# Count matrix of a graph kernel: exact chunk counts through a ring of four slots, and the search for repeats gathered in 14 ranges

## The reference

```python
o = argsort(dst, stable=True)                    # so dst comes sorted, src not
x = x + gat(h, ..., src, dst)                     # sums over the edges of a node
W = zeros((256, 256)).at[src, dst].set(weight)    # edges inside 256 x 256; the last of equal ones wins
x = x + h @ W
x = x + sage(h, edge_index, ...)                  # segment sums of x[src] over dst
x = x + attention(h, edge_index, ...)             # sums exp(...) * h[dst] over src
```

## Time and profile before

| | |
|---|---|
| median of 3 runs | 2122.45 us |
| the profiled execution | 2122.24 us, its span 2120.4 us |
| TensorE matmul | 1728.6 us busy, 82% |
| VectorE | 1583.0 us, 75% |
| ScalarE | 1378.7 us, 65% |
| GpSimd | 303.5 us, 14% |
| changed stage | from about 31 to 319 us |

### The profile page before, as it was taken

One profiled execution on the slowest core, in us unless ns is written; L12 is line 12 of the kernel. 1 busy time (PEld: TensorE's weight loads), 2 busy tenths in 40 slices (PEclk: granted clock), 3 DMA queues, 4 the chain that ended last, 5 costly groups with the idle time before them and its releaser, 6 DMA issues. The chain is left out here.

```text
span 2120.4 us, 63580 instructions
## 1 busy us (share of the span) xinstructions
PE 1728.6 (82%) x21987; PEld 1375.2 (65%) x21987; DVE 1583.0 (75%) x3455; ACT 1378.7 (65%) x2350; POOL 303.5 (14%) x451
## 2 busy tenths in 40 slices
PE   4999985598998737899893699998989985488884
PEld 1333333588888627888883477775548984488883
DVE  7989987899999888999999522222332257899996
ACT  0246885999999659999995622221113354799986
POOL 2466511456500020000000000000000001100000
PEclk9999997799999878999997899999999998699997
DMA  2000000010101000010101200000001010000002
GB/s 84 5 1 2 3 2 27 14 40 28 40 27 40 2 27 30 28 40 27 40 27 50 90 8 0 0 0 7 1 20 36 20 61 14 8 21 28 21 22 99
DMA packets 34799, 54.96 MB, mean 26 GB/s; under 512 B 10668, under 2 KB 26240, under 8 KB 34432
## 3 DMA queue, kind: packets, MB, share of 16 engines
q1 hardware_dynamic: 31232, 51.64, 7.2%
q0 software_dynamic: 3328, 0.06, 0.1%
HBM read 43.19 MB, written 8.49 MB: 24 GB/s over the span
## 5 line engine op out<-in xcount | busy, mean ns | idle before, releaser
L1201 PE MATMUL ps<-R,M 128*128 128x132 f16 (+1 forms) x8640 | 827.1, 222 | 189.7 <-DVE M L1120 112.0
L1201 PEld LDWEIGHTS ps<-R,M 128*128 128x128 f16 x8640 | 763.0, 97 | 218.8 <-issue 115.0
L1075 ACT ACTIVATE Rm<-rows,cB 128x1280 bf16<-128x1280 f32 (+3 forms) x816 | 846.9, 1132 | 31.7 <-DVE Mn L1110 18.4
L1209 PE MATMUL ps<-HB,C 128*128 128x66 f16 x6400 | 590.2, 193 | 0.0
L1209 PEld LDWEIGHTS ps<-HB,C 128*128 128x128 f16 x6400 | 571.6, 97 | 0.0
L1120 DVE TENSOR_TENSOR M<-Rm,C 128x1280 f16<-128x1280 bf16 (+3 forms) x816 | 530.7, 674 | 36.9 <-ACT Rm L1075 29.4
L600 PE MATMUL acc<-ohc,ohl 128*128 128x420 f16 (+1 forms) x1161 | 246.3, 349 | 26.3 <-DVE ohl L564 23.6
L562 DVE TENSOR_SCALAR ohc<-cells,near 128x1280 f16<-128x1280 f16 x387 | 214.3, 554 | 27.9 <-PE acc L600 23.4
L1123 DVE SCALAR_TENSOR_TENSOR M<-rows,cN,C 128x1280 f16<-128x1280 f32 (+1 forms) x144 | 217.3, 1509 | 0.0
L600 PEld LDWEIGHTS acc<-ohc,ohl 128*128 128x128 f16 x1161 | 89.8, 98 | 174.9 <-DVE ohl L564 119.4
L1547 PE MATMUL psA<-R,C 128*128 128x512 f16 (+1 forms) x800 | 144.7, 331 | 9.6 <-DVEq L2036 3.7
(11 more groups left out here) (296 smaller groups left out, 2404.3 us busy)
## 6 DMA issues: line engine op xcount, KB each, us to landing
rows<-rowd SPq DMA_DIRECT2D x32, 640.0 KB, 4.0
rows<-rowd SPq DMA_DIRECT2D x16, 320.0 KB, 3.4
xd<-R SPq DMA_DIRECT2D x4, 640.0 KB, 2.9
xr<-xd SPq DMA_DIRECT2D x20, 128.0 KB, 2.1
xd<-HB SPq DMA_DIRECT2D x1, 2560.0 KB, 8.1
xr<-xd SPq DMA_DIRECT2D x5, 512.0 KB, 6.0
R<-in_x SPq DMA_DIRECT2D x1, 2432.0 KB
xr<-in_x SPq DMA_DIRECT2D x19, 128.0 KB, 2.0
```

Of the source, the lines that this page charges most:

```text
L1075: a.activation(Rm[:, s % SG, 0:wide(p)], rows[:, p % 2, 0:wide(p)], ACT.Relu, bias=cB[:, ds(h + s * nh, 1)]).then_inc(s_R, 1)
L1201: m = pe.matmul(region(p % 2, r), lhsT, rhs, start=first, stop=True, skip_group_check=True)
L1209: m = pe.matmul(both[:, :, cw:2 * cw], C[:, s * NP + p * W + r * P:][:, 0:P], VP[:, s, :, ds(h * cw, cw)], start=False, stop=True, skip_gr ...
```

## The change

Chunks go singly. The table holds the exact number of chunks of a range (three at least), a turn of the loop takes one chunk, and the buffers are a ring of RING = 4 slots whose number is worked out in registers as `(before + i) % RING`, with `before` the number of chunks of earlier ranges. TensorE takes two chunks ahead of the search. The searches are no longer one to a range: the first 14 ranges hold two each (28 in all), the other 26 none. The table of rounds has room for three turns of 28.

```diff
+RING = 4
+SEARCHED = [2] * 14
+NS = sum(SEARCHED)
+TURNS = -(-RND // NS)
...
-                ch(v.tensor_scalar(threes, threes, 1 / U3, 1 / U3, ALU.mult, ALU.add))
-                ch.wait()
-                ch(v.tensor_scalar(table[:, NW:2 * NW], threes, 2.0, None, ALU.max))
-                ch.wait()
-                ch(v.tensor_copy(threes, table[:, NW:2 * NW]))
-                ch.wait()
-                ch(v.scalar_tensor_tensor(table[:, 0:NW], threes, float(PACK), first, ALU.mult, ALU.add))
+                ch(v.tensor_scalar(counts, counts, 3.0, None, ALU.max))
+                ch.wait()
+                ch(v.scalar_tensor_tensor(table[:, 0:NW], counts, float(PACK), first, ALU.mult, ALU.add))
...
-            ohc = ph.sb("ohc", [P, U3, CELLS], f16)
-            ohl = ph.sb("ohl", [P, U3, P], f16)
+            ohc = ph.sb("ohc", [P, RING * CELLS], f16)
+            ohl = ph.sb("ohl", [P, RING * P], f16)
...
+            def slot_of(eng, step):
+
+                return nc.s_assert_within(step % RING, 0, RING - 1, skip_runtime_bounds_check_because="a remainder")
...
-                for q in range(NW):
+                for q in range(NS):
                     w = q % 2
                     with sp.Fori(0, turns) as i:
                         r = round_of(sp, q, i)
...
-                    with v.Fori(0, threes) as i:
-                        for u in range(U3):
-                            k = chunk(first + i * U3 + u, NG * P - 1)
-                            v.wait_ge(s_used, (before + i) * U3 + u + 1)
-                            v.tensor_scalar(ohc[:, u, :], cells[:, :], near[:, q % 2, ds(k, 1)], None,
-                                            ALU.is_equal).then_inc(s_oh, 1)
-                            v.tensor_scalar(ohl[:, u, :], lows[:, :], bT[:, ds(k, 1)], None,
-                                            ALU.is_equal).then_inc(s_oh, 1)
+                    with v.Fori(0, count) as i:
+                        k = chunk(first + i, NG * P - 1)
+                        u = slot_of(v, before + i)
+                        v.wait_ge(s_used, before + i + 1)
+                        v.tensor_scalar(ohc[:, ds(u * CELLS, CELLS)], cells[:, :], near[:, q % 2, ds(k, 1)], None,
+                                        ALU.is_equal).then_inc(s_oh, 1)
+                        v.tensor_scalar(ohl[:, ds(u * P, P)], lows[:, :], bT[:, ds(k, 1)], None,
+                                        ALU.is_equal).then_inc(s_oh, 1)
...
+                    def one(i, opening):
+                        u = slot_of(pe, before + i)
+                        pe.wait_ge(s_oh, (before + i) * 2 + 2)
+                        for b, (d0, d1) in enumerate(DSPLIT):
+                            if opening:
+                                pe.wait_ge(s_out, q * NB + b + 1)
+                            ins = pe.matmul(bank(b, q % 2), ohl[:, ds(u * P, P)], ohc[:, ds(u * CELLS + d0 * NT, (d1 - d0) * NT)],
+                                            start=opening, stop=True, skip_group_check=True)
+                        ins.then_inc(s_used, 1)
+
+                    one(0, True)
+                    one(1, False)
+                    for c in searched(q):
+                        search(c)
+                    with pe.Fori(2, count) as i:
+                        one(i, False)
```

More of the change, by code:

```diff
@@ L477, in first_of, with count_of @@
                                           "the table is built with its first chunk limited to NCH - 1")
-            def threes_of(entry):
-                return nc.s_assert_within(entry // PACK, 2, NCH, skip_runtime_bounds_check_because=
-                                          "the table is built with at least two threes, and no more than cover NCH chunks")
+            def count_of(entry):
+                return nc.s_assert_within(entry // PACK, 3, NCH, skip_runtime_bounds_check_because=
+                                          "the table is built with at least three chunks, and no more than NCH")
+            def slot_of(eng, step):
+                return nc.s_assert_within(step % RING, 0, RING - 1, skip_runtime_bounds_check_because="a remainder")
             @block.gpsimd
@@ L553, in _ @@
                 for q in range(NW):
[L554 removed]
+                    first, count = first_of(coming), count_of(coming)
                     if q + 1 < NW:
@@ L587, in _, with search @@
                 coming, before = packed(pe, 0), 0
+                def search(c):
+                    with pe.Fori(0, turns) as i:
+                        n = turns * c + i
+                        pe.wait_ge(s_sq, n + 1)
+                        hold(pe, s_row[c % 2], turns * (c // 2 * 48) + i * 48 + 48)
+                        pe.matmul(psD[c % 2][:, :], big16[:, :], notlater[:, :, :].rearrange("p u j -> p (u j)"),
+                                  start=True, stop=False)
+                        pe.matmul(psD[c % 2][:, :], left[:, c % 2, :], right[:, c % 2, :], start=False,
+                                  stop=True).then_inc(s_D, 1)
@@ L588, in _ @@
                 for q in range(NW):
-                    threes = threes_of(coming)
+                    count = count_of(coming)
                     if q + 1 < NW:
                         coming = packed(pe, q + 1)
-                    def three(i, opening):
-                        for u in range(U3):
-                            first_ = opening and u == 0
-                            pe.wait_ge(s_oh, (before + i) * (2 * U3) + u * 2 + 2)
-                            for b, (d0, d1) in enumerate(DSPLIT):
-                                if first_:
-                                    pe.wait_ge(s_out, q * NB + b + 1)
-                                ins = pe.matmul(bank(b, q % 2), ohl[:, u, :], ohc[:, u, d0 * NT:d1 * NT],
-                                                start=first_, stop=True, skip_group_check=True)
-                            ins.then_inc(s_used, 1)
@@ L604, in _ @@
-                    three(0, True)
-                    with pe.Fori(0, turns) as i:
-                        n = turns * q + i
-                        pe.wait_ge(s_sq, n + 1)
-                        hold(pe, s_row[q % 2], turns * (q // 2 * 48) + i * 48 + 48)
-                        pe.matmul(psD[q % 2][:, :], big16[:, :], notlater[:, :, :].rearrange("p u j -> p (u j)"),
-                                  start=True, stop=False)
-                        pe.matmul(psD[q % 2][:, :], left[:, q % 2, :], right[:, q % 2, :], start=False,
-                                  stop=True).then_inc(s_D, 1)
@@ L618, in build @@
+                    one(0, True)
+                    one(1, False)
+                    for c in searched(q):
+                        search(c)
+                    with pe.Fori(2, count) as i:
+                        one(i, False)
+                    before = pe.snap(pe.to_reg(before + count), min_val=0, max_val=NW * NCH)
         edge.close()
```

47 lines of the change are left out of this document (23 added, 24 removed).

## The result

The changed kernel takes 2281.19 us (median of 4 runs, 2279.08 to 2284.43) against 2121.72 us (median of 4, 2118.68 to 2123.28): the ratio is 1.0756, 95% interval 1.0739 to 1.0773. It is slower, as forecast; 2268 was predicted, with a range from 2195 to 2325. The profiled execution took 2284.43 us with a span of 2282.2.

A forecast was written before the change was run, and what follows sets the result against it. Queue instructions, hidden under three-chunk turns, were to become the bound: TensorE's 243 us in the first 14 ranges plus VectorE's 180 in the last 26, 423 against 277, +146 on 2122, giving 2268 us, range 2195 to 2325.

The forecast's parts named there:

- What was removed: Count-matrix stage: 353 chunks instead of 387, 34 x 0.625 = 21 us less in comparisons; also 12 of 40 searches.
- a microsecond won or lost here reaches the end one for one: Stage's chunk work, 277.1 us: VectorE's weight sums and an all-engine barrier follow, so changes there reach the end in full.
- stays covered: GpSimd's scatters, which wait for the searches' columns, stay hidden with all searches done by the fourteenth range.
- VectorE's turn: VectorE's one-chunk turn: 0.86 us with old contents plus 0.22 for the slot, taken as 1.09; bounds 0.86 to 1.22.
- the 0.86: VectorE's queue: a turn of one chunk with the old contents, before the slot's arithmetic, taken as 0.86 us.
- TensorE's turn: TensorE's queue: one turn of one chunk takes 0.98 us, including six gaps of 0.06; bounds 0.80 and 1.13.
- nearly free to issue: TensorE's three matmuls a chunk: 0.049 us each by another stage; counted three times, the turn is 1.13, the upper bound.
- The wait for rows: TensorE, between two searches of a range: waits until SP has fetched the second's rows, 1.8 us, 14 times.
- B: Rival: the slot costs nothing, turns of 0.86 and 0.80 us; +75, 2197 us; chance 0.10.
- C: Rival: the sequencers hide behind the comparisons, so the kernel gets faster; -21, 2101 us; chance 0.05.
- D: Rival: only the new wait for rows counts, uncovered; +13, 2135 us; chance 0.03.
- E: Rival: TensorE, half idle in the stage, falls to half clock; +22 on the main forecast, 2290 us; chance 0.10.

The follow-up runs named there:

- threes_ring: The kernel before with only the ring added: four slots worked out in registers for each chunk, turns of three, 387 chunks and 40 searches kept; 2195.23 us, ratio 1.0348.
- masked: The changed kernel with the slot taken by a bitwise and on both engines, and VectorE's `first` worked out once ahead of the loop; 2262.55 us, ratio 1.0662.
- pairs_free: The changed kernel with both waits between a pair's searches removed: rows fetched one search earlier, TensorE waiting for the square before the last; 2248.65 us, ratio 1.0589.
- threes_paired: The kernel before with only the searches changed: two in each of the first 14 ranges, none in the other 26; 2174.59 us, ratio 1.0249.
- singles: The changed kernel with one search in each of the 40 ranges instead of two in 14; 2251.19 us, ratio 1.0608.
- rows_ahead: The changed kernel with SP fetching the rows of a search one search earlier; 2267.92 us, ratio 1.0686.
- early_paired: The kernel before with VectorE's first three ahead of the loop, two searches in the first 14 ranges, rows fetched one search ahead; 2135.62 us, ratio 1.0066.

## Why the prediction was right, and where its terms were off

**The mechanism held.** It said that the queues' register instructions, hidden under three chunks a turn, become the bound with one chunk a turn; that TensorE's queue sets the early ranges and VectorE's the late ones; and that a wait for rows comes between the searches of a pair. Each is there in the trace, and each has a run that moves it: threes_ring shows the slot's arithmetic alone to cost 73.5 us, masked makes both queues cheaper and both parts follow, pairs_free removes the waits and gets 32.5 back. The total missed by 13 us in 159, on the low side.

**What was removed** was read rightly: 34 chunks, 34 x 0.625 = 21 us. The prediction gave no gain for the searches that leave the late ranges, but it had put half of a range's pauses down to the search, and that was wrong: threes_paired won 2.7 us in 26 late ranges without them. Wrong too was "a microsecond won or lost here reaches the end one for one". GpSimd's sum, which "stays covered", had not been covered before: with the last search in the last range it set the start of the next stage, and moving the searches forward won 3.4 us there, a term that the prediction had put at nothing.

**VectorE's turn** was sized at 1.09 us and is 1.00 and 1.02 in turn. The step that was too dear is the slot, 0.22 on top of 0.86; it was 0.14 to 0.16, if the 0.86 holds, which no run measured. The compiler made one instruction of 271 ns and one of 53 of it, not the 350 to 400 that the prediction looked for. With the measured turn the prediction's own sum gives 152 x 1.01 + 26 x 0.53 = 167 us for the late part, where 168.0 were measured and 180 predicted.

**TensorE's turn** was sized at 0.98 and is 1.085, between that and the upper bound of 1.13. The register instructions and the branch are 0.60 us of the turn (115 + 36 + 2 x 46 for L622, 56 + 73 + 227 for L630), near the 0.62 of the prediction. Too small was what lies around them: 0.49 us instead of six gaps of 0.06. One gap more is there, since the instructions are seven; whether the rest is the three matmuls, "nearly free to issue", or longer gaps, the rows don't tell. With 1.085, 201 x 1.085 - 3 + 24 = 239 us, and the early part of pairs_free takes 238.3.

**The wait for rows** was sized at 1.8 us and cost 2.44 a pair, by pairs_free. Half of the difference is a slip in the prediction: it counted the search's 0.87 us from the start of the second matmul, 129.86, and so had TensorE ready at 130.7. Without a wait the second search starts 0.83 us after the first one's first matmul (pairs_free), which would be 130.38 there, 0.3 earlier. From SP's last issue to TensorE's start the prediction had 1.04 us (131.46 to 132.5), and ten of the 14 pairs have 1.11 to 1.15. The other four are longer, up to 1.64, for a reason that wasn't looked for. With it 239 + 14 x 2.44 = 273 for the early part of the changed kernel, measured 272.5.

So the early part's 272.5 against the predicted 243 goes back to TensorE's turn (0.10 x 201 = 20 us) and the rows' wait (0.65 x 14 = 9), and the late part gave 12 back. Two terms too small and one too large left 17.6 us in the chunk work of the profiled execution (440.6 against 423). The stage's end took 3.4 of them back, and the median, 3 under that execution, is 13 above the forecast. That it came so close is in part luck: errors of 29 and of 12 + 3 us point opposite ways.

**The rivals.** B, a slot for nothing, was refuted by threes_ring; a power of two as the divisor doesn't make it free. masked shows that written as a mask it costs a little less: some 7 us by TensorE's queue, and on VectorE part of the 9.6 us of the late part, since `first` was moved out of the loop there too. C, the sequencers hidden behind the comparisons, came out with the wrong sign; it is also what the Trainium skill's rule of occupancy ("Perfetto Trace Analysis", Identifying the Most-Contended Engine) gave. This case's traces don't bear it out: VectorE was the busy engine, it lost 16 us of `ohc` comparisons, and the chunk work grew by 163. D, only the wait, is the 32.5 us of pairs_free. E is half right: the half clock did come, but by another cause than the one named. The prediction had it from a TensorE half idle all along; pairs_free, without pauses, keeps 1.00 over its ranges with pairs. And it cost the changed kernel next to nothing: eleven matmuls at half clock took 4.10 us, 1.12 a chunk against 1.085.

**The parts of +159.5 us**, by the runs: fewer chunks -21 (353 instead of 387 at 0.625); the waits inside the pairs +32.5 (after less pairs_free); the slot some +67 (0.19 of threes_ring on 353 chunks, an estimate, since in another turn it may cost otherwise); the stage's end -3.4; the remaining 84 are the turn for every chunk, with 28 searches that now lie on the queue that sets the pace (27 of them by the 0.98 from singles and pairs_free). How the turn and the slot share the rest was argued, not shown: no run had one chunk a turn with fixed slots.

## What to carry to other kernels

Before a loop's turn is made smaller, add up its queue instructions, each with the gap around it, for each engine that runs the loop, and compare a turn with the work that it issues: busy shares won't show it, and the profile names another engine as the releaser. Before two uses of a resource are put together, follow the chain that must pass between them; two buffers don't help while a semaphore still counts as with one, and behind each wait removed ask for the next. At a stage's end look for the engine that comes last to the barrier; it needn't be the one that sets the pace of the loop. Take what lies at a range's start off the path by placing it under the work of the same engine, but only on the engine that is late there.

## What the runs showed of the hardware

- Around each queue instruction of VectorE lie some 0.07 us beyond its duration: six of them with 0.598 us of durations made a turn of 0.996. One more instruction of 45 ns, and 16 ns more in the others, made a turn 0.095 us longer (0.89 to 0.98 in masked).
- On TensorE's queue the instruction with the slot took 115 ns with a remainder and 79 with a mask.
- A taken branch took 227 ns on TensorE's queue and 56 on VectorE's.
- Behind TensorE's pauses of 2.3 to 2.9 us in the kernel after, from the second pair on, the granted clock over the next 4 us was 0.50 to 0.80; in threes_paired, with pauses of 2.35 to 3.04 us, it was 0.50 to 0.67 behind ten of thirteen and 1.00 behind three. With pauses of 1.2 us it was 0.91 over the ranges with pairs in rows_ahead and 0.99 in early_paired. With the pauses removed it was 1.00 over 181 us in pairs_free.
- TensorE, waiting for three small transfers, went on 1.11 to 1.15 us after SP had issued the last of them in ten of 14 pairs, and up to 1.64 in the other four; the bytes in the GB/s row had made it look like 0.9.
- From the end of GpSimd's sum to the next stage behind the barrier it was 6.13 or 6.14 us in four kernels, from the end of VectorE's last sum 0.85 or 0.86 in the eight others.
